# Second attention of a fused two-layer block: row quantisation divided over more passes of its loop

## What is computed

```python
def _rms_norm(x):
    return x * jax.lax.rsqrt(jnp.mean(jnp.square(x), axis=-1, keepdims=True) + RMS_EPS)

def _act_quant(x):
    scale = 127.0 / jnp.maximum(jnp.max(jnp.abs(x), axis=-1, keepdims=True), 1e-05)
    return jnp.clip(jnp.round(x * scale), -128.0, 127.0) / scale

def bit_linear(x, w):          # weights quantised to -1, 0, 1
    xn = _rms_norm(x)
    xq = _ste(xn, _act_quant(xn))
    wq = _ste(w, _weight_quant(w))
    return jnp.einsum('bni,oi->bno', xq, wq)
...
q = bit_linear(x, wq); k = bit_linear(y, wk); v = bit_linear(y, wv)
scores = q @ k.T (16 query heads, 8 key heads, head size 16); attn = softmax(scores); out = attn @ v
out = layernorm(out) * ln_gamma + ln_beta
x = x + bit_linear(out, wo)      # the last four lines in short form
```

## Time and profile before

| | before |
|---|---|
| median of 3 runs | 1782.86 us (1780.49 to 1787.54) |
| profiled execution, time | 1780.72 us |
| its span, first to last instruction | 1778.9 us |
| mean granted TensorE clock | 0.856 |
| busy: PE / DVE / ACT / POOL | 76% / 72% / 58% / 43% |
| second attention's loop, T0 to T62 | 624.33 to 908.11 us of the span |

### The profile page before, as it was taken

The page is one execution under the profiler, slowest core; times in us unless marked ns, Lnnn a source line. Parts: engine busy times, 40 slices in busy tenths (PEclk is TensorE's granted clock), DMA queues, the critical chain, the costliest instruction groups (busy, mean ns, idle before and its releaser), DMA issues. The chain is left out here.

```text
span 1778.9 us, 33549 instructions
## 1 busy us (share of the span) xinstructions
PE 1352.1 (76%) x12580; PEld 769.0 (43%) x12580; DVE 1285.0 (72%) x2324; ACT 1023.1 (58%) x1851; POOL 764.4 (43%) x808
## 2 busy tenths in 40 slices
PE   6999347988679887778845837344788789799898
PEld 4544123655544355555532312002345445355566
DVE  3698899961368675777667739999999899985200
ACT  2676335433444476777653447433798798885553
POOL 2355000000232434434414016656788788877443
PEclk9999668999779988788967868556899899899999
DMA  6496200000145576687512358997564465560000
GB/s 261 160 356 264 80 0 0 1 1 0 67 148 166 173 136 121 116 145 127 82 34 89 99 134 207 248 222 199 139 164 115 120 163 130 125 148 8 1 13 13
DMA packets 152516, 212.37 MB, mean 119 GB/s; under 512 B 107199, under 2 KB 112255, under 8 KB 139296
## 3 DMA queue, kind: packets, MB, share of 16 engines
q1 hardware_dynamic: 152356, 210.23, 46.1%
HBM read 155.37 MB, written 31.75 MB: 105 GB/s over the span
## 5 line engine op out<-in xcount | busy, mean ns | idle before, releaser
L2782 POOL TENSOR_TENSOR mf_st<-mf_st,mf_c_rep 128x1024 f32<-128x1024 f32 x128 | 301.3, 2354 | 202.5 <-DVE mf_st L2850 202.5
L2850 DVE TENSOR_TENSOR_SCAN mf_st<-mf_dA,mf_u_ps 128x512 f32<-128x512 f32 x256 | 309.9, 1211 | 0.0
L2673 PE MATMUL mf_y_ps<-mf_st,c_consts 128*32 128x512 f32 x512 | 130.0, 735 | 135.0 <-POOL mf_st L2782 99.1
L2961 ACT ACTIVATE mf_dA<-c_dt,c_neg_a 128x496 f32<-128x496 f32 x256 | 163.8, 699 | 69.1 <-DVE mf_st L2850 68.2
L2844 DVE TENSOR_TENSOR mf_u_ps<-mf_st,mf_b_ps 128x512 f32<-128x512 f32 x256 | 177.7, 694 | 21.5 <-DMA mf_st<-xs 10.6
L2805 POOL TENSOR_TENSOR mf_hid<-mf_g,mf_hid 128x512 f16<-128x512 f32 x128 | 148.3, 1159 | 95.9 <-ACT mf_g L2978 95.9
L2975 ACT ACTIVATE mf_hid<-mf_eh,c_vecs 128x512 f16<-128x512 f32 x128 | 87.9, 687 | 122.4 <-PE mf_eh L2724 121.9
L2724 PE MATMUL mf_eh<-mf_parts,mf_w 128*128 128x512 f16 x480 | 125.0, 399 | 19.6 <-POOL mf_parts L2801 18.0
L259 POOL TENSOR_TENSOR c_parts<-mg_ln_hT,c_parts 128x512 f16<-128x512 f32 x8 | 9.0, 1156 | 302.6 <-ACT c_parts L250 302.5
L2111 DVE TENSOR_REDUCE t_mx<-t_s_ps 128x2 f32<-128x514 f32 x128 | 87.8, 687 | 56.9 <-PE t_s_ps L1997 56.8
L2057 ACT ACTIVATE t_p<-t_s_ps,t_mx 128x257 f32<-128x257 f32 x256 | 107.2, 476 | 20.2 <-DVE t_mx L2111 18.2
(11 more groups left out here) (510 smaller groups left out, 2998.7 us busy)
## 6 DMA issues: line engine op xcount, KB each, us to landing
mf_st<-xs SPq DMA_DIRECT2D x64, 1024.0 KB, 7.2
a_ctx_t<-in_ctx_t SPq DMA_DIRECT2D x16, 1024.0 KB, 9.0
a_ctx_n<-in_ctx_n SPq DMA_DIRECT2D x16, 1024.0 KB, 8.0
cqs<-a_whole_rows SPq DMA_DIRECT2D x16, 512.0 KB, 6.7
mo_raw<-in_l_w SPq DMA_DIRECT2D x16, 512.0 KB, 4.0
ws<-mo_split SPq DMA_DIRECT2D x32, 256.0 KB, 2.6
c_cq<-cqs SPq DMA_DIRECT2D x16, 512.0 KB, 5.1
mf_w<-ws SPq DMA_DIRECT2D x20, 256.0 KB, 11.6
```

The lines of the kernel that those rows point to most:

```text
L2673: m = e.matmul(y_ps[T * j:T * j + T, :], c.pick[:, gg, :], st[u % RING][:, j, :], start=(gg == 0), stop=(gg == 3))
L2782: e.tensor_tensor(half(u, h), half(u, h), over(c_rep[u // UNITS % 2][:, :], [P, 2, BT], 1), ALU.mult).then_inc(hcs("done"), 1)
L2850: e.tensor_tensor_scan(st[u % RING][:, j, :], dA[:, n % AHEAD, :], u_ps[j % 2][:, :], 0.0, ALU.mult, ALU.add).then_inc(hs("done"), 1)
L2961: e.activation(by_batch(dA[:, n % AHEAD, :])[:, :, 1:], dt, ACT.Exp, scale=c.neg_a[:, at:at + 1]).then_inc(dAs("done"), 1)
```

## The change

The steps of both chains are divided further and placed in other passes. Lags, as (query chain; output chain, counted from its start):

| step | before | after |
|---|---|---|
| moments / std | 0 / 1; 0 / 1 | the same |
| norm (output chain: gain, then norm) | 2; 2 and 2 | 2; 2 and 3 |
| squares / root (ScalarE) | 3 / 3; 3 / 3 | 3 / 4; 4 / 5 |
| scale / integers (VectorE) | 4 / 4; 4 / 4 | 5 / 6; 6 / 7 |
| transpose of the integers (SyncE) | 5; 5 | 7; 8 |
| rows and drain, two halves | 7, 8; 7, 8 | 8, 9; 9, 10 |
| round and low part | 9; - | 10; - |
| send, two parts | 10, 11; - | 11, 12; - |

The third output chain now ends behind the loop: its integers and their transpose come after pass 63.

```diff
--- before.py
+++ after.py
@@ -1254,6 +1254,12 @@
 
 def quantise(e, own, rt, ints, r, factor, i):
 
+    quantise_scale(e, own, rt, r, factor, i)
+    quantise_ints(e, own, ints, r)
+
+
+def quantise_scale(e, own, rt, r, factor, i):
+
     e.tensor_reduce(r.amax[:, :], r.xn[:, :, :], AX.X, ALU.max, apply_absolute_value=True).then_inc(*own())
     e.wait_ge(*own.now())
     e.wait_ge(*rt.at("done", i))
@@ -1266,6 +1272,10 @@
     e.tensor_scalar(r.scale[:, :], r.scale[:, :], 127.0, None, ALU.mult).then_inc(*own())
     e.tensor_scalar(r.f[:, :], r.factor[:, :], factor, None, ALU.mult).then_inc(*own())
     e.wait_ge(*own.now())
+
+
+def quantise_ints(e, own, ints, r):
+
     for k in range(KT_):
         e.tensor_scalar(r.big[:, k, :], r.xn[:, k, :], r.scale[:, k:k + 1], ROUND, ALU.mult, ALU.add).then_inc(*own())
     e.wait_ge(*own.now())
@@ -1278,8 +1288,16 @@
 
 
 def row_rt(e, squares, rt, r, junk, i, c):
+    row_squares(e, squares, r, junk)
+    row_root(e, squares, rt, r, i, c)
+
+
+def row_squares(e, squares, r, junk):
     for k in range(KT_):
         e.activation(junk[:, k, :], r.xn[:, k, :], ACT.Square, accum_out=r.ss[:, k:k + 1]).then_inc(squares("done"), 1)
+
+
+def row_root(e, squares, rt, r, i, c):
     e.wait_ge(*squares.at("done", i))
     e.activation(r.rt[:, :], r.ss[:, :], ACT.Sqrt, scale=1.0 / C, bias=c.eps[:, 1:2]).then_inc(rt("done"), 1)
 
@@ -1787,7 +1805,7 @@
         rows_t, drained = done(sem, "rows_t"), done(sem, "drained")
         q_turned, x_turned, q_sent = sem("q_turned"), sem("x_turned"), sem("q_sent")
         block = ctx.enter_context(nc.Block())
-        GROUPS = B // BPT
+        GROUPS, PAST = B // BPT, 4
 
         def query(b, lag):
 
@@ -1801,11 +1819,11 @@
 
         def extras(b):
 
-            return ([("q", query(b, 7 + h), h) for h in range(2) if query(b, 7 + h) > 0] +
-                    [("x", project_out(b, 7 + h), h) for h in range(2) if project_out(b, 7 + h) >= 0])
+            return ([("q", query(b, 8 + h), h) for h in range(2) if query(b, 8 + h) > 0] +
+                    [("x", project_out(b, 9 + h), h) for h in range(2) if project_out(b, 9 + h) >= 0])
 
         ring = []
-        for b in range(B + 2):
+        for b in range(B + PAST):
             ring += extras(b)
         ring += [("x", BLOCKS - 1, 0), ("x", BLOCKS - 1, 1)]
         turn_of = {tile: n for n, tile in enumerate(ring)}
@@ -1888,19 +1906,22 @@
                     load(b // BPT + 4)
                 if b % BPT == 0 and b // BPT + 2 < GROUPS:
                     fetch(b // BPT + 2)
-                if query(b, 5):
-                    turn_queries(query(b, 5))
+                if query(b, 7):
+                    turn_queries(query(b, 7))
                 for x in range(2):
-                    if query(b, 10 + x):
-                        send(query(b, 10 + x), x)
-                if project_out(b, 5) >= 0:
-                    turn_attended(project_out(b, 5))
+                    if query(b, 11 + x):
+                        send(query(b, 11 + x), x)
+                if project_out(b, 8) >= 0:
+                    turn_attended(project_out(b, 8))
                 if b % BPT == 2 and b > BPT:
                     move(b // BPT - 1)
                 if b >= 2 * BPT:
                     place(b // BPT - 2, b % BPT)
                 if b % BB == 3 and b > BB and b // BB + 1 < BLOCKS:
                     fetch_last(b // BB + 1)
+            for b in range(B, B + PAST):
+                if project_out(b, 8) >= 0:
+                    turn_attended(project_out(b, 8))
             for w in range(BPT):
                 place(GROUPS - 2, w)
             move(GROUPS - 1)
@@ -1952,8 +1973,8 @@
                 end(b)
                 if b + LEAD < B:
                     split(b + LEAD)
-                if query(b, 9):
-                    low_query(query(b, 9))
+                if query(b, 10):
+                    low_query(query(b, 10))
 
         @block.tensor
         def _(e):
@@ -2071,13 +2092,13 @@
                     e.activation(copy_of(q_parts[0], dup), qn[:, :, :].rearrange("p k (c d) -> p (k c) d", d=HD),
                                  ACT.Copy).then_inc(q_rounded("done"), 1)
 
-            def query_rt(i):
+            def query_squares(i):
                 e.wait_ge(*q_normed.at("done", i - 1))
-                row_rt(e, q_squares, q_rt, qr, junk, i - 1, c)
-
-            def attended_rt(i):
+                row_squares(e, q_squares, qr, junk)
+
+            def attended_squares(i):
                 e.wait_ge(*x_normed.at("done", i))
-                row_rt(e, x_squares, x_rt, xr, xjunk, i, c)
+                row_squares(e, x_squares, xr, xjunk)
 
             for s in (*exps, *kept, q_std, q_squares, q_rt, q_rounded, x_std, x_squares, x_rt):
                 s.start(e)
@@ -2093,15 +2114,20 @@
                 if query(b, 1):
                     row_std(e, q_var, q_std, qr, query(b, 1) - 1, c)
                 if query(b, 3):
-                    query_rt(query(b, 3))
-                if query(b, 9):
-                    round_query(query(b, 9))
+                    query_squares(query(b, 3))
+                if query(b, 4):
+                    row_root(e, q_squares, q_rt, qr, query(b, 4) - 1, c)
+                if query(b, 10):
+                    round_query(query(b, 10))
                 if project_out(b, 1) >= 0:
                     row_std(e, x_var, x_std, xr, project_out(b, 1), c)
-                if project_out(b, 3) >= 0:
-                    attended_rt(project_out(b, 3))
+                if project_out(b, 4) >= 0:
+                    attended_squares(project_out(b, 4))
+                if project_out(b, 5) >= 0:
+                    row_root(e, x_squares, x_rt, xr, project_out(b, 5), c)
             row_std(e, x_var, x_std, xr, BLOCKS - 1, c)
-            attended_rt(BLOCKS - 1)
+            attended_squares(BLOCKS - 1)
+            row_root(e, x_squares, x_rt, xr, BLOCKS - 1, c)
 
         @block.vector
         def _(e):
@@ -2149,22 +2175,28 @@
                 e.wait_ge(*q_squares.at("done", i - 2))
                 normalise(e, own, q_std, q_normed, qr, q_tiles(i), i - 1)
 
+            def query_scale(i):
+                e.wait_ge(*q_normed.at("done", i - 1))
+                quantise_scale(e, own, q_rt, qr, c.wf[:, 0:1], i - 1)
+
             def query_ints(i):
-                e.wait_ge(*q_normed.at("done", i - 1))
                 if i > 1:
                     e.wait_ge(q_turned, (i - 1) * 16)
-                quantise(e, own, q_rt, q_ints, qr, c.wf[:, 0:1], i - 1)
+                quantise_ints(e, own, q_ints, qr)
 
             def attended_stats(i):
                 e.wait_ge(placed[i], BB * 16)
                 moments(e, own, x_var, xr, x_tiles(i))
 
-            def attended_norm(i):
+            def attended_gain(i):
                 r = xr
                 e.wait_ge(*x_squares.at("done", i - 1))
                 for k in range(KT_):
                     e.scalar_tensor_tensor(r.big[:, k, :], x_tiles(i)[:, k, :], r.mean[:, k:k + 1], c.row["x_gamma"],
                                            ALU.subtract, ALU.mult).then_inc(*own())
+
+            def attended_norm(i):
+                r = xr
                 e.wait_ge(*own.now())
                 e.wait_ge(*x_std.at("done", i))
                 e.reciprocal(r.rstd[:, :], r.std[:, :]).then_inc(*own())
@@ -2173,11 +2205,14 @@
                     e.scalar_tensor_tensor(r.xn[:, k, :], r.big[:, k, :], r.rstd[:, k:k + 1], c.row["x_beta"],
                                            ALU.mult, ALU.add).then_inc(x_normed("done"), 1)
 
+            def attended_scale(i):
+                e.wait_ge(*x_normed.at("done", i))
+                quantise_scale(e, own, x_rt, xr, c.wf[:, 3:4], i)
+
             def attended_ints(i):
-                e.wait_ge(*x_normed.at("done", i))
                 if i:
                     e.wait_ge(x_turned, i * 16)
-                quantise(e, own, x_rt, x_ints, xr, c.wf[:, 3:4], i)
+                quantise_ints(e, own, x_ints, xr)
 
             def drain(n):
                 kind, i, h = ring[n]
@@ -2220,20 +2255,31 @@
                     moments(e, own, q_var, qr, q_tiles(query(b, 0)))
                 if query(b, 2):
                     query_norm(query(b, 2))
-                if query(b, 4):
-                    query_ints(query(b, 4))
+                if query(b, 5):
+                    query_scale(query(b, 5))
+                if query(b, 6):
+                    query_ints(query(b, 6))
                 if project_out(b, 0) >= 0:
                     attended_stats(project_out(b, 0))
                 if project_out(b, 2) >= 0:
-                    attended_norm(project_out(b, 2))
-                if project_out(b, 4) >= 0:
-                    attended_ints(project_out(b, 4))
+                    attended_gain(project_out(b, 2))
+                if project_out(b, 3) >= 0:
+                    attended_norm(project_out(b, 3))
+                if project_out(b, 6) >= 0:
```

(8 more changed lines are left out.)

## The result

The changed kernel takes **1808.08 us** (median of 4 runs, 1805.84 to 1810.57) against 1785.20 us (4 runs, 1780.49 to 1789.89): ratio **1.0112, interval 1.0085 to 1.0139**. The forecast was slower, 1796 us in 1774 to 1809. The profiled execution took 1810.57 us with a span of 1808.7; before it was 1780.72 and 1778.9. These two executions are 29.85 us apart, where the medians are 22.9: the profile after is of the slowest of its four runs. What follows by stretches describes these two executions, and is some 7 us more than the medians show.

The account below looks back on a forecast made before the run. A ring was taken to bound the second attention's loop: scores, maxima, exponentials, next scores. Terms -11.6, +7.2, +4.8, +9.4, +1.5, +0.4, +4.0 sum to +15.7 on 1780.7: 1796 us, range 1774 to 1809.

Parts of the forecast that it names:

- the two waits: Loop: TensorE's projection waits for its rows, +7.2 query, +4.8 output chains; scores wait for keys behind both sends, +9.4.
- passes 9 to 14: Rounding, low part and sends a pass later delay the key transposes: +9.4 us, bounds -8 and +13.
- the collisions: Output chain's integers share pass 32 with query moments, drains the norm of pass 34, scale lengthens 31 and 47: +1.5 us.
- the clock: TensorE idling at five new projection waits lowers its granted clock: +4.0 us, bounds 0 and 8.
- Query passes: Passes 3 to 8 of three query chains, row work cut into smaller pieces: -11.6 us, bounds -14 and 0.
- the measured pair carries as much work: Passes 17 and 18, 8.04 us, hold a ScalarE root and VectorE norm; taken as price, 8.0, per new query pair.
- The table loads: ScalarE's root: priced from the trace, 1.28 us a load; by the skill's 2.66 us the sum would be +24.
- The end: Last output chain: passes 59 to 61 -3.7, later root, transpose and `move` +4.1; together +0.4 us.
- relief wins: Rival: shorter ScalarE runs win in the loop, TensorE and SyncE absorb projection and sends; about -17, 1763 us; chance 0.16.

Follow-up runs that it names:

- The first experiment, turned-rows-first kernel: Changed kernel with SyncE issuing the transpose of the integers ahead of the key transpose of its pass, nothing else: 1801.08 us, 1.0067.
- relieved kernel: Changed kernel with the integers' transpose ahead of the keys, rounding and low part back in pass 9, sends in passes 10 and 11: 1786.28 us, 1.0006.
- two merged forms: Changed kernel with squares and root together again: 1812.53 us, 1.0135; separately, changed kernel with scale and integers together again: 1819.71 us, 1.0174.

## Why the prediction was right, and where it was off

The direction, the two waits and the range were right, the range narrowly: 1808.08 lies 1 us inside its upper end, and the profiled execution 1.6 us outside. The gain was priced too high, and the cost of passes 9 to 14, the collisions and the clock too low. By stretches, forecast against the two profiled executions:

- **Direction and the two waits.** The projection stands for its rows in all three query chains, 8.3 us forecast as 7.2; for the output chain 3.67 us in pass 50 and some 0.5 in pass 34, forecast as 4.8. The first experiment took them away.
- **Passes 9 to 14: +14.3 us, forecast +9.4.** The mechanism is shown by the kernel before with only these moves (+13.0 there). The 13.3 us from key transpose to key transpose were 12.64. What was mis-sized is the rest: at a granted clock of 0.74, 0.68 and 0.73 all three came out at 35 us, where I had 32.5 and 34.0; which instructions take the difference was not tested. The 91.15 us before hold a stall of 3.12 us (last section) that the changed kernel's have not, so the moves cost up to that much more.
- **Query passes: the step that failed.** I forecast -11.6 ahead of the waits; measured is 86.95 - 8.3 - 82.37 = -3.7, and -5.4 in the relieved kernel. By pairs of the changed kernel: passes 3 and 4 take 8.23, 7.80 and 7.39 us, as forecast (8.0); passes 7 and 8 without the wait 7.75 on the mean, as forecast (7.6). Passes 5 and 6 take 10.71, 10.06 and 11.21 instead of 8.0, three times 2.7 us. The failed step is "the measured pair carries as much work". The 8.04 us of the pair 17 and 18 are a pass of 2.94 and one of 5.10:

```profile
697.44 0.41 PE L1997 MATMUL t_s_ps<-t_kT,c_qT 32*32 32x258 f16 x16
...
699.20 0.69 DVE L2111 TENSOR_REDUCE t_mx<-t_s_ps 128x2 f32<-128x514 f32 x1
```

```profile
699.20:702.14 2.94, 2.19 (x101) 1.50 (x101) 2.88 (x8) 1.94 (x5) 1.22 (x3) 1.00 1.12 195
702.14:707.24 5.10, 3.11 (x109) 2.15 (x110) 3.55 (x9) 5.04 (x9) 1.65 (x5) 0.98 0.46 94
```

  Pass 17 holds no chain step of VectorE, and is shorter than a light pass (3.79) because it starts late: its scores were done at 697.85, but VectorE was in the moments of pass 16, and its maximum began straight behind them, at 699.20. In the changed kernel pass 5, with root and scale, takes 5.73, 5.51 and 5.46 us, 0.5 more than pass 18 on the mean. Pass 6, with the integers, takes 4.98, 4.55 and 5.75, some 2.2 more than pass 17. In passes 5 and 6 of the changed kernel:

```profile
649.41:660.12 10.71, 8.28 (x222) 5.65 (x223) 8.75 (x23) 8.65 (x17) 3.48 (x11) 0.84 0.67 112
730.74:740.80 10.06, 7.62 (x217) 5.02 (x217) 8.84 (x23) 8.61 (x17) 3.82 (x12) 0.81 0.94 171
814.84:826.05 11.21, 8.84 (x217) 5.63 (x218) 8.94 (x23) 8.14 (x16) 3.86 (x12) 0.68 1.03 185
```

  VectorE's 8.8 us are 2.4 more than the 6.43 of the pair 17 and 18, since scale and integers are 4.0 us of work and the norm there is 1.6. ScalarE's piece, a root with two table loads, is the same in both pairs. Pass 21 is held by it: the exponentials go behind the root and its two table loads, and the scores behind them 1.02 us late:

```profile
731.34 1.28 ACT L1302 ACT_TABLE_LOAD   x1
732.64 0.30 ACT L1302 ACTIVATE t_rtq<-t_ssq,c_eps 128x4 f32<-128x4 f32 x1
...
733.44 1.28 ACT L2078 ACT_TABLE_LOAD   x1
734.73 0.84 ACT L2078 ACTIVATE t_p<-t_s_ps,t_mx 128x257 f32<-128x257 f32 x2
...
735.72 0.41 PE L2018 MATMUL t_s_ps<-t_kT,c_qT 32*32 32x258 f16 x16 [1.02 <-ACT t_p L2078]
```

  VectorE works without a break up to the end of the scale, at 736.06, but these scores are done only at 736.13, so the scale costs next to nothing here. What holds pass 6 was not separated further; the integers, 2.0 us of VectorE, are what is new in it.

  The prediction said itself that the quantising was covered by ScalarE's run, and then priced the integers, which have no cover now, by a pass that held no such work.
- **The table loads.** Root and exponentials start 1.30 and 1.29 us after the start of their loads, with nothing between, so the trace decides as it did before. The Trainium skill (ScalarE: Activation LUTs, "What ACT_TABLE_LOAD costs") gives about 2.66 us with a drain; the trace does not agree.
- **Collisions: +5.5 us, forecast +1.5.** Passes 15 to 18 are 2.2 us longer, 31 to 34 3.7 and 50 to 56 3.9, less the 4.2 us of the output chain's waits counted above. No experiment separates them further.
- **The end: -1.8 us, forecast +0.4.** Passes 59 to 61 take 10.6 us (-5.1, forecast -3.7). The last combining comes 8.77 us behind T62 instead of 6.61 (+2.2, forecast +1.4); `move` is issued 4.4 us later against T62 (forecast +4.1), and what follows T62 is 3.3 us longer:

```profile
943.39 0.43 DVE L2160 TENSOR_TENSOR t_tot<-t_o_ps,t_tail 128x272 f32<-128x272 f32 x1
```

```profile
946.83 0.43 SPq L1883 DMA_DIRECT2D shift<-t_on  x1
```

- **Clock: +4 us was too little.** I priced five passes. The loop has some 44 us more at the lower level. Pass 14 spent 3.5 us there (at 0.62) and lost 0.8, so 0.23 us for each: an estimate of 10 us, spread over the stretches above and not to be added to them.

With the 3.1 us ahead of T0 the terms as measured, -3.7 + 8.3 + 4.2 + 14.3 + 5.5 - 1.8 + 3.1, give 29.9 against 29.85 of the two executions. With the pairs of passes 5 and 6 priced as measured (8 us more) the forecast would have been 1804. Of the rivals, "relief wins" asked for both waits to vanish. Where they do, in the relieved kernel, the time is that of before, not 1763, though that kernel has the new overlap of GpSimd and VectorE told there.

## What to carry to other kernels

When work that several engines do side by side is cut into more passes, ask for each piece what ran beside it: a piece that was covered must be priced at its full length once its cover moves. A measured "pass pair" is a price only if the engines carry the same work in it and its start is not late; here such a pair was 2.7 us too cheap.

When a chain is lengthened, the moves of its transposes and of what they serve must be equal. Here a distance of one pass instead of two cost 2.6 to 3.7 us in four of five places, and 0.5 in the fifth. Rounding, low part and both sends, one pass later, cost 11 us in the kernel before with nothing else changed. Mending the two places gave 8 and 5 us apart and 15 together.

After every move, look at what now runs beside it. In the relieved kernel two VectorE instructions of 0.16 us became 2.0 us each beside GpSimd's low part, and no wait of VectorE shows it, since they count as busy.

## What the runs showed that was not expected

**A stall that no wait explains.** In some executions TensorE stands for about 3 us before an instruction whose inputs are there. Of the kernel before and the relieved kernel:

```profile
739.31 0.37 PE L2007 MATMUL t_pt_ps<-c_consts,t_p 128*128 128x128 f32 x1 [3.12 <-issue]
```

```profile
741.44 0.38 PE L2001 MATMUL t_kv_ps<-c_wkv,c_xT 128*128 128x256 bf16 x2 [3.63 <-issue]
```

The turned-rows-first kernel has one of 3.43 us. Each comes soon after a context transpose was issued. The DMA queues show one packet of kind "instruction" in the window of each stall (664 to 668.2 us in the turned-rows-first kernel), but so does the window 700 to 704 us of the kernel before, which has no stall. That TensorE's instructions come late behind the transpose's packets would fit, but is not shown. It matters here because such stalls, 2.9 to 3.8 us where they occur, are as large as the effects looked for, and the profiles of the changed kernel and of its two merged forms have none of this length.

**Waits seem to cost twice.** Of the 23.4 us that the loop grew, 16.3 are the same matmuls taking longer at a granted clock of 0.79 instead of 0.85, and only 7 are more idle time of TensorE, as far as the modelled ends go. The relieved kernel, with the projection waits gone, is back at 0.84 over a loop of 286.4 us. That the waits lowered the clock is what these three kernels suggest; no run changed the clock alone.
